# Gated cross-attention with routed experts: expert weights as scaled 16-bit halves, six experts resident instead of three

## The reference

```python
x = x + tanh(g_xattn) * xattn(ctx, layernorm(x), mask, ...)
# xattn: q = lat @ Wq; k, v = concat(layernorm(ctx), lat * gate) @ Wk, Wv
#        softmax(q k / 8, masked) v @ Wout
h = layernorm(x)
bids = sigmoid(h @ conf_w.T + conf_b) * wealth
top_bids, chosen = top_k(bids, 2);  w = softmax(top_bids)
ffn_e(h) = (silu(h @ gate_e.T) * (h @ up_e.T)) @ down_e.T      # 1024 wide
x = x + tanh(g_ffn) * sum_over_chosen(w_e * ffn_e(h))
```

## Time and profile before

| | |
|---|---|
| time, median of 3 runs | 1637.66 us (1635.76 to 1641.44) |
| span of the profiled execution | 1632.5 us; its own time is not on record, the median lies 5.2 us above this span |
| PE busy | 1429.1 us, 88% |
| DVE busy | 953.5 us, 58% |
| ACT busy | 843.4 us, 52% |
| POOL busy | 599.9 us, 37% |
| granted TensorE clock, mean | 0.971 |
| DMA | 180.57 MB, mean 111 GB/s |

### The profile page before, as it was taken

One profiled execution on the slowest core, in us unless ns is written; L12 is line 12 of the kernel. 1 busy time (PEld: TensorE's weight loads), 2 busy tenths in 40 slices (PEclk: granted clock), 3 DMA queues, 4 the chain that ended last, 5 costly groups with the idle time before them and its releaser, 6 DMA issues.

```text
span 1632.5 us, 39655 instructions
## 1 busy us (share of the span) xinstructions
PE 1429.1 (88%) x11944; PEld 1084.8 (66%) x11945; DVE 953.5 (58%) x2651; ACT 843.4 (52%) x1873; POOL 599.9 (37%) x666
## 2 busy tenths in 40 slices
PE   0599989998999899989998659999999999999956
PEld 0266656665666565656565447888888778888845
DVE  3388888888888888888887634233332223333311
ACT  3377777777777777777776422223332223333311
POOL 3244544654465446543653321222222222222211
PEclk9899999999999999999999869999999999999987
DMA  3124234423342344233423387411113771111183
GB/s 97 49 78 153 92 107 135 162 91 108 133 162 91 110 132 162 91 111 130 162 79 110 142 262 220 132 29 26 29 26 82 239 220 26 29 26 29 26 256 82
DMA packets 70907, 180.57 MB, mean 111 GB/s; under 512 B 11664, under 2 KB 33552, under 8 KB 70864
## 3 DMA queue, kind: packets, MB, share of 16 engines
q1 hardware_dynamic: 54464, 153.66, 28.2%
q0 software_dynamic: 15264, 24.25, 7.6%
q10 hardware_dynamic: 1136, 2.12, 0.5%
HBM read 106.91 MB, written 73.09 MB: 110 GB/s over the span
## 4 chain that ended last, share of the span: by engine, by line
PE 63%; DVE 13%; issue 9%; DMA 8%; ACT 2%; POOL 1%; another core or an unknown queue 1%; SPq 1%; DVEq 1%; POOLq 0%; ACTq 0%
PE fP L1203 15%; PE yP L1203 10%; PE gP L1203 9%; PE uP L1203 9%; PE simP L1251 4%; DMA W<-split_experts 4%; PE ptP L1261 3%; PE oP L1203 3%; PE aP L1387 3%; PE tP L1203 3%; DMA out<-ysb,xt 2%; DVE pT L864 2%; DMA xt<-routed_rows 1%; DVE ms L858 1%
## 5 line engine op out<-in xcount | busy, mean ns | idle before, releaser
L1142 DVE TENSOR_TENSOR act_h<-uP,sg 128x512 f32<-128x512 f32 x126 | 87.1, 691 | 290.4 <-ACT sg L756 290.4
L1203 PE MATMUL fP<-zTs,ws 128*128 128x112 f16 (+1 forms) x1536 | 220.6, 294 | 25.6 <-DVE kT L848 13.0
L1203 PE MATMUL gP<-W,xT 128*128 (+1 forms) x756 | 212.2, 417 | 33.3 <-issue 26.1
L756 ACT ACTIVATE sg<-gP 128x512 f32<-128x512 f32 x126 | 75.4, 598 | 290.8 <-PE uP L1203 289.0
L858 DVE CUSTOM_DVE_ANT_0 ms<-simP,madd,sim_undo 112x488 f32<-112x488 f32 x256 | 184.7, 722 | 37.1 <-remote 19.8
L557 POOL DMA_INDIRECT out<-ysb,xt x63 | 100.6, 1597 | 271.7 <-ACT ysb L768 256.3
L1203 PEld LDWEIGHTS yP<-W,aT 128*128 128x128 f32 x1512 | 191.1, 193 | 10.1 <-issue 5.3
L1203 PE MATMUL yP<-W,aT 128*128 (+1 forms) x1512 | 192.9, 284 | 4.7 <-DVE aT L1146 4.7
L1203 PE MATMUL uP<-W,xT 128*128 (+1 forms) x756 | 196.0, 395 | 0.0
L1203 PE MATMUL fP<-ws,zTs 128*128 128x512 f16 x768 | 186.9, 379 | 10.3 <-DVE kT L848 10.1
L656 ACT ACTIVATE pr<-ms,nmax 112x488 f32<-112x488 f32 x256 | 179.2, 700 | 31.4 <-DVE nmax L858 27.6
(11 more groups left out here) (204 smaller groups left out, 2261.3 us busy)
## 6 DMA issues: line engine op xcount, KB each, us to landing
split_experts<-wparts SPq DMA_DIRECT2D x32, 1536.0 KB, 6.6
W<-split_experts SPq DMA_DIRECT2D x64, 768.0 KB
wr<-wffn SPq DMA_DIRECT2D x32, 768.0 KB, 8.0
xc<-ctxt SPq DMA_DIRECT2D x32, 375.0 KB
xt<-routed_rows POOLq DMA_DIRECT2D x63, 129.0 KB, 2.4
xl<-x SPq DMA_DIRECT2D x32, 112.0 KB
xres<-x SPq DMA_DIRECT2D x32, 112.0 KB, 7.8
out<-x SPq DMA_DIRECT2D x32, 112.0 KB, 1.9
```

The costliest lines, as they stand in the source:

```text
L756: nc.scalar.activation(sg[i][:, :], gP[i][:, :], ACT.Silu).then_inc(s_silu, 1)
L1142: nc.vector.tensor_tensor(act_h[i][:, :], uP[i][:, :], sg[i][:, :], ALU.mult).then_inc(s_act, 1)
L1203: last = nc.tensor.matmul(o, lhs(k, a), rhs(k, c), start=n == 0, stop=n == len(todo) - 1)
```

## The change

The experts' weights, the routed rows and the activations become float16 halves. To fit float16's range they are scaled: in bodies 0 to 13 SP loads the weights a first time, in halves of an expert (128x3072), and ACT sums their squares (`scan_half`, twice a body, in steps 4 and 7); POOL keeps the largest (`fold_sums`), and after body 13 makes the scales from them (`fit_weights`). In bodies 14 to 29 SP loads the weights again, ACT scales them in place (`scale_half`, in steps 4 and 7), POOL splits them (`split_weights`, now two pieces of 128x1536 in a body), and SP stores them. `W2` holds six experts in float16, its places used from the last to the first, an expert is loaded in 6 chunks, and the scales are undone in the operations of the expert part; `weigh` moves from ACT to DVE.

```diff
-SLOTS = 3
+SLOTS = 6
...
-WLD, WAHEAD = 8, 2
+WLD, WAHEAD = 6, 2
...
-    wsp = nc.dram_tensor("split_experts", (E, P, 2, WCOL), F32).ap()
+    wsp = nc.dram_tensor("split_experts", (E, P, 2, WCOL), F16).ap()
...
+        wstage = [sb(f"wstage{i}", [P, WHALF], F32, pa) for i in range(2)]
+        wparts = sb("wparts", [P, 2, WHALF], F16, pa)
...
-        W2 = sb("W2", [P, SLOTS, 2, WCOL], F32R, pb)
-        xT = [sb(f"xT{i}", [P, 2, KD, P], F32R, pb) for i in range(2)]
+        xT = [sb(f"xT{i}", [P, 2, KD, P], F16, pb) for i in range(2)]
+        W2 = sb("W2", [P, SLOTS, 2, WCOL], F16, pb)
...
+            def load_half(p, e):
+
                 apart(sp)
-                sp.dma_start(wstage, wffn[bass.ds(e, 1), :, q * WCH:(q + 1) * WCH].rearrange("a p c -> (a p) c")).then_inc(s_wst, 16)
-
-            def put_weights(e, q):
-                sp.wait_ge(s_wlo, e * WPB + q + 1)
+                sp.dma_start(wstage[p][:, :], wffn[bass.ds(e, 1), :, p * WHALF:(p + 1) * WHALF].rearrange("a p c -> (a p) c")).then_inc(s_wst[p], 16)
...
+            def put_half(p, e):
...
+                sp.dma_start(wsp[bass.ds(e, 1), :, :, p * WHALF:(p + 1) * WHALF].rearrange("a p h c -> (a p) h c"),
+                             wparts[:, :, :]).then_inc(s_wput, 16)
...
+                if scan_e is not None:
+
+                    need(sp, s_wscan, (b - 1) * 2)
+                    load_half(p, scan_e)
+                if put_e is not None:
+
+                    sp.wait_ge(s_wlo, (b - 2 * E - 1) * 2)
+                    put_half(p, put_e)
+                if split_e is not None:
+                    load_half(p, split_e)
...
+            with sp.Fori(E + 1, PAIRS) as j:
+                turn_of(j * 2, 0, put_e=j - (E + 1), split_e=j - E)
+                turn_of(j * 2 + 1, 1, put_e=j - (E + 1), split_e=j - E)
...
-                    sp.dma_start(W2[:, n % SLOTS, :, c * step_:(c + 1) * step_].bitcast(F32),
+                    sp.dma_start(W2[:, SLOTS - 1 - n % SLOTS, :, c * step_:(c + 1) * step_],
...
-            sp.wait_ge(s_wput, 16 * B)
-            sp.wait_ge(s_pv, H * (B - 1))
-            sp.wait_ge(s_plo, seq(B - 2, NPIECE))
+            sp.wait_ge(s_wput, 16 * (NHALF + 1))
...
-            load_expert(2)
+            for n in range(2, SLOTS):
+                load_expert(n)
...
+            def fold_sums(n, p):
+
+                pool.wait_ge(s_wscan, n * 2 + 2)
+                need(pool, s_wfold, n)
                 apart(pool)
-                nc.gpsimd.tensor_copy(wparts[:, 0, :], wstage).then_inc(s_whi, 1)
-                pool.wait_ge(s_whi, b + 1)
-                apart(pool)
-                nc.gpsimd.tensor_tensor(wparts[:, 1, :], wstage, wparts[:, 0, :].bitcast(F32), ALU.subtract).then_inc(s_wlo, 1)
+                nc.gpsimd.tensor_scalar(wmax[:, :], wmax[:, :], wsum[:, p, 0:1], wsum[:, p, 1:2], ALU.max, ALU.max).then_inc(s_wfold, 1)
...
+            def fit_weights():
...
+                pool.wait_ge(s_wfold, NHALF)
+                pool.dma_start(wsum_d[0:1, :].rearrange("a p -> p a"), wmax[:, :]).then_inc(s_wall, 16)
+                pool.wait_ge(s_wall, 16)
+                pool.dma_start(wall[:, :], wsum_d[0:1, :].to_broadcast([P, P])).then_inc(s_wall, 16)
+                pool.wait_ge(s_wall, 32)
+                w = P // 2
+                while w:
+                    link(nc.gpsimd.tensor_tensor(wall[:, 0:w], wall[:, 0:w], wall[:, w:2 * w], ALU.add))
+                    w //= 2
...
+            def split_weights(b, p):
+
+                n = (b - 2 * (E - 1)) * 2
+                need(pool, s_wput, (b - (2 * E - 3)) * 16)
+                for q in range(2):
+                    o = slice(q * WPIECE, (q + 1) * WPIECE)
+                    pool.wait_ge(s_wscl, n + (q + 1))
+                    apart(pool)
+                    nc.gpsimd.tensor_copy(wparts[:, 0, o], wstage[p][:, o]).then_inc(s_whi, 1)
...
+                    nc.gpsimd.tensor_tensor(wparts[:, 1, o], wstage[p][:, o], wparts[:, 0, o], ALU.subtract).then_inc(s_wlo, 1)
...
+            with pool.Fori(1, E - 1) as j:
+                body(j * 2, 0, j, fold=True)
+                body(j * 2 + 1, 1, j, fold=True)
+            fit_weights()
+            pool.sem_inc(s_wput, 16)
+            with pool.Fori(E - 1, PAIRS - 2) as j:
+                body(j * 2, 0, j, split=True)
+                body(j * 2 + 1, 1, j, split=True)
...
+            def scan_half(n, p, q):
...
+                nc.scalar.activation(wstage[p][:, o], wstage[p][:, o], ACT.Square, accum_out=wsum[:, p, q:q + 1]).then_inc(s_wscan, 1)
+
+            def scale_half(n, p, q):
...
+                act.wait_ge(s_wfit, 1)
+                o = slice(q * WPIECE, (q + 1) * WPIECE)
+                nc.scalar.activation(wstage[p][:, o], wstage[p][:, o], ACT.Copy, scale=wfit[:, 0:1]).then_inc(s_wscl, 1)
+
+            def body(b, p, last_pair=None, scan=False, scale=False):
                 for h in range(H):
+                    if h in (4, 7):
+                        if scan:
+                            scan_half(b + 2, p, h // 7)
+                        if scale:
+                            scale_half(b + 2, p, h // 7)
...
-                nc.vector.tensor_tensor(xT[q][:, 1, :, :], xP[:, :, :], xT[q][:, 0, :, :].bitcast(F32), ALU.subtract).then_inc(s_xtlo, 1)
+                nc.vector.scalar_tensor_tensor(out=xT[q][:, 1, :, :], in0=xP[:, :, :], scalar=X_TOP, in1=xT[q][:, 0, :, :],
+                                               op0=ALU.mult, op1=ALU.subtract).then_inc(s_xtlo, 1)
...
+            def weigh(t, k):
+
+                dve.wait_ge(s_down, t + 2)
+                need(dve, s_add, (t - 1) * 16)
+                nc.vector.tensor_scalar(ysb[k % 2][:, :], yP[:, :], xt[k][:, D + 1:D + 2], wfit[:, 3:4], ALU.mult, ALU.mult).then_inc(s_yw, 1)
```

More of the change, by code:

```diff
@@ L730, in _ @@
                 norm_rows(1, 1, part)
+            for q in range(2):
+                scan_half(0, 0, q)
             for n in range(NPIECE):
@@ L738, in _ @@
                 norm_rows(2, 0, part)
-            body(0, 0)
-            body(1, 1)
-            with act.Fori(1, PAIRS - 2) as j:
-                body(j * 2, 0, j - 1)
-                body(j * 2 + 1, 1, j - 1)
+            for q in range(2):
+                scan_half(1, 1, q)
+            body(0, 0, scan=True)
+            body(1, 1, scan=True)
+            with act.Fori(1, E - 1) as j:
+                body(j * 2, 0, j - 1, scan=True)
+                body(j * 2 + 1, 1, j - 1, scan=True)
+            with act.Fori(E - 1, PAIRS - 2) as j:
+                body(j * 2, 0, j - 1, scale=True)
+                body(j * 2 + 1, 1, j - 1, scale=True)
             for b in range(B - 4, B + 2):
-                body(b, b % 2)
+                body(b, b % 2, scale=b < B - 2)
             def tile_hi(t, q):
                 act.wait_ge(s_xtp, t + 1)
-                nc.scalar.activation(xT[q][:, 0, :, :], xP[:, :, :], ACT.Copy).then_inc(s_xthi, 1)
+                nc.scalar.activation(xT[q][:, 0, :, :], xP[:, :, :], ACT.Copy, scale=X_TOP).then_inc(s_xthi, 1)
             def silu(t, i):
@@ L762, in act_hi @@
                 nc.scalar.activation(aT[q][i][:, 0, :, :], aP[i][:, :, :], ACT.Copy).then_inc(s_athi, 1)
-            def weigh(t, k):
-                act.wait_ge(s_down, t + 2)
-                need(act, s_add, (t - 1) * 16)
-                nc.scalar.activation(ysb[k % 2][:, :], yP[:, :], ACT.Copy, scale=xt[k][:, D + 1:D + 2]).then_inc(s_yw, 1)
             def step(t, k):
@@ L781, in step @@
                     act_hi(t, q, 0)
-                if holds(t, 1, NT):
-                    weigh(t - 1, (k - 1) % 4)
             tile_hi(0, 0)
@@ L1159, in step @@
                     act_lo(t, q, 0)
+                if holds(t, 1, NT):
+                    weigh(t - 1, (k - 1) % 4)
             def tile_table():
```

121 lines of the change are left out of this document (70 added, 51 removed).

## The result

The changed kernel takes 1648.23 us (median of 5 runs, 1647.73 to 1652.17) where the kernel before takes 1635.76 (1630.95 to 1641.44) in runs beside it: a ratio of 1.0087, 95% interval 1.0063 to 1.0111. It is slower by about 14 us by the ratio; 11 us faster was forecast. The time lies inside the stated range of 1598 to 1658 us, but on the other side of the kernel before. The profiled execution has a span of 1646.5 us, 14.0 above that of before and 25.0 above the 1621.5 at which the prediction's sum arrives before it adds 5.2 us for what lies outside the span; that execution took 1648.17 us, so that the addition was 1.7 here.

What follows compares the result with a forecast made beforehand. In attention PE was taken as nearest the bound, DVE and ACT close behind; in the expert part PE is busy without a gap. 1632.5 − 82 gains + 71 costs = 1621.5, plus 5.2 outside the span: 1627 us, range 1598 to 1658.

Steps and rivals of the forecast that it cites:

- Products: Expert part: 16-bit products make a tile .55 us shorter; over 62 tiles −34 us (0 to −45).
- The stalls at the end: Expert part, near the end: six places remove two PE waits, 12.07 and 10.61 us, and the half clock behind them; −27 us.
- The chain on POOL: Bodies 14 to 29: two cast-subtraction pairs make rstd late, ACT stands 4.4 us in seven even bodies; +31 us.
- Contention: Second half: DVE operations beside POOL's longer work are drawn out, 1 us in each of seven pairs; +7 us (0 to +40).
- Rival D: Bodies 14 to 29: DVE's two-input routing operations pay contention with POOL, 40 us instead of 7; 1660 us; chance .10.
- Insertions on ACT: Bodies 2 to 29: four new operations a pair cost 1.2 us, +18; first-half DVE waits give −8; net +10 us.
- The fit of the scales: After body 13: POOL's chain with two small transfers delays the next rstd; +6 us, above about 11.41.
- The start: First loads: scan transfers among them +5, four insertions on ACT 7; +12 us (+4 to +31).
- B: POOL's splits: cast to 16 bits goes at the subtraction's pace, 2.0 us longer each; 1655 us; chance .14.
- C: Second half: the forecast ACT stall does not show, 31 + 5 us fall away; 1590 us; chance .22.
- E: Expert part: 16-bit products are no faster, +34 us, a tile taking 9.4; 1661 us; chance .04.
- F: Attention part: all of ACT's insertions show on PE, 6 us a pair in place of 1.2; 1699 us; chance .05.

Runs made afterwards that it cites:

- run 6: PE's loop over expert tiles has 8 tiles in a turn in place of 4, on the changed kernel: 1642.73 us, ratio 1.0043 to the kernel before.
- run 7: Expert weights have three places on the chip in place of six, else the changed kernel: 1660.26 us, ratio 1.0132 to the kernel before.
- run 12: Changed kernel with ACT scaling 8 of 1536 columns in each second-half scaling operation: 1637.9 us, ratio 1.0079 to the kernel before.
- run 13: Changed kernel with POOL's second cast and subtraction in odd second-half bodies cut to 8 of 1536 columns: 1621.1 us, ratio 0.9963 to the kernel before.
- run 14: Changed kernel with both the edits of run 12 and run 13: 1604.77 us, ratio 0.9869 to the kernel before.
- run 11: Changed kernel with only the choice of experts on VectorE moved to steps 3 and 4: 1649.04 us, ratio 1.0076 to the kernel before.
- run 3: Changed kernel with the first of two POOL splits put ahead of the scatter in odd second-half bodies: 1656.65 us, ratio 1.0176 to the kernel before.
- run 5: Changed kernel with POOL doing rstd and rstd1 ahead of mask_bias and rows_lo in even second-half bodies: 1641.52 us, ratio 1.0028 to the kernel before.
- run 10: Kernel of run 5 with POOL's subtraction replaced by two memsets of about the same size: 1621.2 us, ratio 0.9902 to the kernel before.
- run 1: Changed kernel with ACT's scans and scalings ahead of steps 3 and 4 in place of 4 and 7: 1632.18 us, ratio 1.0025 to the kernel before.
- run 2: Changed kernel with the fit cut in pieces between POOL's operations and body 14's scalings both in step 7: 1639.1 us, ratio 1.0062 to the kernel before.
- run 4: Changed kernel with first scans ahead of normalized rows and the first expert-weight load after the first attention loads: 1630.38 us, ratio 1.0012 to the kernel before.

## Why the prediction was wrong, point by point

**Products: right.** 8.89 us a tile against 8.9; yP's products .109 each (2.62 us for 24) against .110. (The .72 in the bound of this term follows from none of its rows.) What the sum missed is the turn of the loop: four tiles took 38.4 us, 0.5 over four times 9.46, and take 36.8 now, 1.2 over four times 8.89, which over 14 turns takes 9 us off the gain; run 6 got 1.2 back for each turn saved. By luck as much was added by four tiles in the middle part, slow before (10.6 to 13.8 us) and at full pace after, of which the forecast had 4.

**The stalls at the end, the first expert, the last bodies: right in sum.** −63.8, −5.2 and −9.2 for −65, −5 and −10.8. The reason given for the end, the six places, is some 10 of its 27 us; by run 7 the halved bytes gave the rest.

**"The chain on POOL": right in kind, and its sum in part by luck.** 3.6 us of waiting for 4.4, 47.3 us in the second half for 51.4. Runs 12 and 13 show that it is this order that sets the pair, and that the 8.4 us added there for ACT's insertions are not a second item. The wait alone would be 25 us, 31 in the forecast; a pair is 6.9 us longer, not 3.6. With POOL's order relieved 3.3 come back (run 13) and with ACT's scalings thin too 5.0 (run 14); the terms for insertions, contention and clock, 20 us, filled this gap without being its cause one by one. "Contention" was put at 1 us a pair beside it; run 11 shows that its one hold costs nothing as long as POOL's order is the bound, and runs 3, 5 and 10 that holds are what comes next, up to 3 us at a time. Rival D priced it as an addition and not as the next bound. The Trainium skill (SBUF — State Buffer, "Who interferes with whom") says that the side that comes second is blocked until the other's instruction is over; run 3 agrees, where VectorE's 2.95 us end at 670.50 and the subtraction's 3.09 at 670.48. The rule on two inputs in SBUF, by which the prediction marked off what is caught, was too narrow for these runs: the longest holds of runs 3 and 5 are of `TENSOR_SCALAR`, which has one input tensor.

**The step that failed is "Insertions on ACT", in its credit.** It gave back 8 us in the first half because DVE's waits "released by nothing the profile names" might go once POOL had no split. They did not: it is 27.5 us in 14 turns after, for 19.8. Nothing tied it to POOL. In six pairs of the first half these waits come to 8.0 us in the kernel before, so that "may partly go" had been priced as if all of it went. The runs show that they go with the chip or the hour of a run (the two were not varied apart) and not with the split: they are there in both halves of every trace where the kernel before takes 1636 to 1637 us, and in none where it takes 1627, split or no split. And 1.2 us a pair was too little for what an insertion in step 7 of each body costs, although the place had been named: 1.5 by run 1; the pair grew by 2.0, of which 0.7 is the growth of the unnamed wait. Together 12.8 us.

**"The fit of the scales" failed as well, in its path and in its size**, 6 us for 16.5. The term looked for the cost in the next `rstd` behind the fit on POOL. The cost came by ACT, whose first scaling needs the scale and stands 11.78 us for it in step 4 of body 14; no term had this wait. The size was bounded by the wait for first loads, 11.41 us; the two transfers in sequence are 12.4, the arithmetic is a chain of 15 small operations behind them, 4.4, and PE falls to half clock after 11.37 us of standing. Another 10.5 us. Run 2 brought 8 of the pair's 17.7 back.

**The start** was 3.3 us more than forecast; run 4 shows that nearly all of it is the order of loads and scans.

These three come to 26.6 us, where 25.0 lie between forecast and measurement; the other stages cancel to −1.6. None of the rivals is what happened: the cast took 1.46 us (B), the stall was there (C), the line of `bids<-bids,confb` had a median of 1.2 us in the second half (D), a tile took 8.89 us (E), and insertions cost 2 of the 6 us a pair of F. What stays open: what releases DVE's ms in the unnamed waits, how the 8 us of run 2 divide, and the last 2 us of a second-half pair in run 14.

## What to carry to other kernels

An insertion is priced by the stretch in which it stands: 1.7 us where idle time followed delayed one operation and nothing behind it, and where none followed they cost 0.75 to 1.0 a body, with the same total load on the engine. A value that is made late must be asked for late: look for its first reader on every engine, not only for what stands behind its maker. A wait is only credited as gone if a row ties it to what is removed. Where two engines' orders each bound a loop, price the larger alone and name the other as what remains once it is mended: here the two repairs of the second half, each by itself, gave nothing (run 3) or a third of the wait (run 5). All repairs in one kernel made it 2.7% faster than before.
